# A state-space layer on Trainium2: next quarter's layer norm and half its input projection recorded inside the scan

## What is computed

```python
x = x + mamba(layernorm(x))        # state-space layer
x = x + ffn(layernorm(x))          # binarized weights
x = x + attn(layernorm(x))         # 16 x 16 scores of heads, per position
x = x + ffn(layernorm(x))

def mamba(x):                      # one sequence: 2048 x 1024
    xb, zb = split(x @ in_proj_w)  # 2048 x 2048 each
    xb = silu(causal_conv4(xb) + conv_b); zb = silu(zb)
    dt, B, C = split(xb @ x_proj_w)            # 128, 16, 16 wide
    dt = softplus(dt @ dt_proj_w + dt_proj_b)
    h[t] = exp(dt*A) * h[t-1] + dt*B[t]*xb[t]  # 2048 channels, 16 states each
    y = sum over states of h*C, plus xb*D
    return (y * zb) @ out_proj_w
```

## Time and profile before

| | us |
|---|---|
| median of 2 timed runs | 7102.89 (7080.65 and 7125.14) |
| profiled execution, slowest core | 7031.2 |
| its span, first to last instruction | 7029.7 (the eight cores 6995.0 to 7029.7) |
| VectorE busy | 3376.6 (48%) |
| TensorE matmul busy | 2594.3 (37%) |
| ScalarE busy | 1388.7 (20%) |
| GpSimd busy | 389.4 (6%) |

### The profile page before, as it was taken

The page is one execution under the profiler, slowest core; times in us unless marked ns, Lnnn a source line. Parts: engine busy times, 40 slices in busy tenths (PEclk is TensorE's granted clock), DMA queues, the critical chain, the costliest instruction groups (busy, mean ns, idle before and its releaser), DMA issues.

```text
span 7029.7 us, 35317 instructions; the slowest of 8 cores (6995.0 to 7029.7 us)
## 1 busy us (share of the span) xinstructions
PE 2594.3 (37%) x9120; PEld 935.0 (13%) x9120; DVE 3376.6 (48%) x3380; ACT 1388.7 (20%) x2282; POOL 389.4 (6%) x204
## 2 busy tenths in 40 slices
PE   3211115111134111152111200397833433436978
PEld 1000002000011000010000000143311111112433
DVE  0377771577753677735777640101155565563011
ACT  1122221222222222212222202212010100101120
POOL 1000000000000000000000011000002212211000
PEclk8655558555557555576555555698966666667989
DMA  6300005000011000021000069632400000001414
GB/s 111 65 0 0 0 0 92 29 0 0 0 27 45 24 0 0 0 55 41 0 0 0 19 106 118 89 75 45 87 0 0 0 0 0 0 0 22 81 41 109
DMA packets 691335, 226.16 MB, mean 32 GB/s; under 512 B 680122, under 2 KB 680253, under 8 KB 687552
## 3 DMA queue, kind: packets, MB, share of 16 engines
q1 hardware_dynamic: 555552, 168.14, 10.4%
q0 software_dynamic: 135584, 55.76, 7.0%
HBM read 241.73 MB, written 37.88 MB: 40 GB/s over the span
## 4 chain that ended last, share of the span: by engine, by line
DVE 39%; PE 25%; ACT 14%; DMA 12%; issue 6%; DVEq 2%; POOL 1%; ACTq 0%; SPq 0%; POOLq 0%; PEldq 0%
DVE AR L640 17%; ACT AR L613 10%; PE ps L881 6%; PE ps L851 5%; DVE AR L626 5%; DVE AR L1018 4%; DVE AR L1058 3%; DVE AR L1011 2%; DVE AR L492 2%; PE ps L1086 2%; PE ps L985 2%; PE ps L464 2%; PE ps L301 2%; DMA AR<-ip_bf 2%; DMA AR<-w 1%
## 5 line engine op out<-in xcount | busy, mean ns | idle before, releaser
L665 PE MATMUL ps<-AR 128*128 128x512 bf16 x1024 | 517.8, 608 | 2468.8 <-DVE AR L656 2468.8
L640 DVE TENSOR_TENSOR_SCAN AR<-AR 128x1024 bf16<-128x1024 f32 x512 | 1173.5, 2292 | 40.7 <-issue 3.8
L613 ACT ACTIVATE AR<-AR 128x511 f32<-128x511 f32 x1024 | 674.0, 705 | 1.1 <-issue 0.8
L626 DVE TENSOR_TENSOR AR<-AR 128x1024 bf16<-128x1024 bf16 x512 | 354.6, 693 | 485.2 <-ACT AR L613 485.2
L851 PE MATMUL ps<-AR 128*128 128x512 bf16 x2048 | 457.5, 384 | 126.1 <-DVE AR L336 111.7
L649 ACT ACTIVATE AR<-AR 128x2 f32<-128x2 bf16 x512 | 104.7, 204 | 1924.6 <-DVEq L63 1924.6
L1086 PE MATMUL ps<-AR 128*128 128x512 bf16 x512 | 220.7, 587 | 659.8 <-POOL AR L1072 635.0
L665 PEld LDWEIGHTS ps<-AR 128*128 128x128 bf16 x1024 | 70.0, 104 | 2915.0 <-issue 2915.0
L888 DVE TENSOR_SCALAR AR<-ps,AR 128x1024 f32<-128x1024 f32 x32 | 43.0, 1344 | 861.8 <-PE ps L881 861.8
L881 PE MATMUL ps<-AR 128*128 128x512 bf16 x2048 | 449.8, 383 | 12.7 <-DMA AR<-w2s 12.7
L656 DVE TENSOR_TENSOR AR<-AR 128x1024 bf16<-128x1024 bf16 x512 | 354.3, 692 | 127.7 <-issue 127.7
(11 more groups left out here) (92 smaller groups left out, 2340.6 us busy)
## 6 DMA issues: line engine op xcount, KB each, us to landing
AR<-w1s SPq DMA_DIRECT2D x128, 256.0 KB, 3.0
AR<-w2s SPq DMA_DIRECT2D x32, 1024.0 KB, 6.6
AR<-ip_bf SPq DMA_DIRECT2D x96, 256.0 KB, 2.9
AR<-bc_hbm SPq DMA_DIRECT2D x4, 4096.0 KB, 12.0
AR<-op_bf SPq DMA_DIRECT2D x24, 512.0 KB, 4.3
X<-x_fm SPq DMA_DIRECT2D x1, 8192.0 KB, 28.6
AR<-in_proj_w POOLq DMA_DIRECT2D x32, 256.0 KB, 5.2
ip_bf<-AR SPq DMA_DIRECT2D x32, 256.0 KB, 3.0
```

The source lines that it names most:

```text
L613: nbase=nbase: e.activation(out=dec_all[gb][:, n, 1:TQ], in_=dt[b][:, 1:TQ], func=AF.Exp, scale=av[:, dd, nbase + n:nbase + n + 1]),
L626: e.tensor_tensor(out=inp_all[0], in0=v[b].unsqueeze(1) .broadcast_to([128, G, TQ]), in1=bbc[:, nbase:nbase + G, :], op=ALU.mult))
L640: e.tensor_tensor_scan(out=h_all[hb].rearrange("p a b -> p (a b)"), data0=dec_all[gb].rearrange("p a b -> p (a b)"), data1=inp_all[0].rear ...
L665: e.matmul(self.bank(b, TQ), self.ident[:], hc_all[hb][:, n, :], start=(ng == 0 and n == 0), stop=(ng == NG - 1 and n == G - 1)),
```

## The change

The body of `_mamba` is divided into functions: `do_ln`, `inproj_block`, `do_conv`, `do_xproj`, `do_scan`, `do_outproj`. Quarter 0 is led in by layer norm, all 32 projection blocks, convolution and x-projection. Then, for each quarter q, the scan of q is recorded together with a list of "pieces": the layer norm of quarter q+1 and its projection blocks 0 to 15, 17 pieces in all. After each `groups(dd-1)` two pieces are recorded. After the scan come output projection q, projection blocks 16 to 31 of q+1, its convolution and x-projection. The barrier at the end of each quarter is gone; one stands at the end of the stage. Waits name the counts that they need. The rest follows from that or is small:

- Layer norm takes its scratch from xbpre instead of the tile of B and C, and accumulates in banks 4 and 5; dt and v get memory of their own; the gated output is written over zbs, and g is gone; x-projection uses bank 5 instead of 6.
- TensorE's wait for the small weights (x_proj_w, dt_proj_w) moves to the begin of the stage.
- The wait for the broadcast load (d_spb) moves from ahead of the scan into each group; the prologue gets a wait xbs_ready, the end of a channel block zb_ready, each projection block xn_ready. For the first two blocks of each projection half SP waits for its own last DMA on the buffer (sp_par).
- Drains are removed: in layer norm, after L730 and L895, in the weight preparation, and in attention after L1018, L1058 and ahead of three increments (`r.inc` has a drain of its own).
- In attention the tiles sc, am, sm get two buffers each instead of one.

```diff
-    def _layernorm(self, t0, tlen, xn_view, o_ln):
+    def _layernorm(self, t0, tlen, xn_view, o_ln, bb=0, bb2=2, waits=None):
...
-        o_g = o_xbpre
...
-        o_dt = o_xn
-        o_v = o_xn + 2 * TQ * 4
+        o_dt = alloc(2 * TQ * 4)
+        o_v = alloc(2 * TQ * 2)
...
-        o_ln = o_bbc
+        o_lnm = o_xbpre
...
         r.wait("gp", "d_gpb", small_w)
+        r.wait("pe", "d_gpb", small_w)
...
+        def do_ln(qq):
+            lv = max(st.get("ln_ve", 0), st.get("conv_ve", 0))
+            ln_waits = [("act", "c_ve", lv), ("pe", "c_ve", lv)]
+            self._layernorm(qq * TQ, TQ, xn, o_lnm, bb=4, bb2=5,
+                            waits=ln_waits)
+            st["xn_ready"] = r.cnt["c_ve"]
+            st["ln_ve"] = r.cnt["c_ve"]
+            st["ln_evac"] = r.cnt["c_act"]
+
+        def inproj_block(qq, m, mm_done, ev_done, wr_done, dst):
+            b = m % 2
+            if qq == 0:
...
+            else:
+                if m >= 2:
+                    r.wait("sp", "c_pe", mm_done[m - 2])
+                if m in (0, 1, 16, 17):
+                    r.wait("sp", dsem("sp", b), st["sp_par"][b])
+                ddone = r.op("sp", lambda e, m=m, b=b: e.dma_start(
+                    out=wi[b], in_=d["ip_bf"][:, m * 128:(m + 1) * 128]
+                    .rearrange("(k p) f -> p k f", p=128)),
+                     inc=dsem("sp", b), inck=16)[dsem("sp", b)]
+                st["sp_par"][b] = ddone
+                r.wait("pe", dsem("sp", b), ddone)
+            r.wait("pe", "c_ve", st["xn_ready"])
+            if m >= 2:
+                r.wait("pe", "c_act", ev_done[m - 2])
+            else:
+                r.wait("pe", "c_act", st["ln_evac"])
+                r.wait("pe", "c_ve", st["ln_var"])
+            for k in range(8):
+                c = r.op("pe", lambda e, m=m, b=b, k=k: e.matmul(
+                    self.bank(4 + b, TQ), wi[b][:, k, :], xn[:, k, :],
+                    start=(k == 0), stop=(k == 7)),
+                         inc="c_pe" if k == 7 else None)
+            mm_done[m] = c["c_pe"]
+            r.wait("act", "c_pe", mm_done[m])
+            if m < 16:
+                c = r.op("act", lambda e, m=m, b=b: e.activation(
+                    out=xbpre[:, m, 3:3 + TQ], in_=self.bank(4 + b, TQ),
+                    func=AF.Copy), inc="c_act")
+            else:
+                r.wait("act", "c_pe", st.get("op_mm", 0))
...
-            bc_done = r.cnt["d_spb"]
-            r.wait("gp", "d_spb", bc_done)
-            r.wait("ve", "d_spb", bc_done)
-            r.wait("pe", "c_act")
...
             def prologue(dd):
...
                 r.wait("ve", "c_act", dt_ev[b])
-                if dd >= 2:
-                    r.wait("ve", "c_gp", inp_done[(dd - 2, NG - 1)])
+                r.wait("ve", "c_act", xbs_ready)
...
             def groups(dd):
...
                     r.wait("ve", "c_act", dec_done[key])
-                    inp_done[key] = r.cnt["c_gp"]
+                    r.wait("ve", "d_spb", bc_done)
                     if dd + ng > 0:
                         sem, val = hc_done.get(keyp2, ("c_ve", 0))
                         r.wait("ve", sem, val)
...
                 r.wait("ve", "c_pe", ymm_done[(dd, NG - 1)])
+                r.wait("ve", "c_act", zb_ready)
...
-                ep_done = r.op("ve", lambda e, dd=dd, b=b: e.tensor_tensor(
-                    out=g[:, dd, :], in0=yv[b], in1=zbs[:, dd, :],
+                ep_done[0] = r.op("ve", lambda e, dd=dd, b=b: e.tensor_tensor(
+                    out=zbs[:, dd, :], in0=yv[b], in1=zbs[:, dd, :],
                     op=ALU.mult), inc="c_ve")["c_ve"]
...
                     prologue(dd)
                 if dd >= 1:
                     groups(dd - 1)
...
-                r.drain("ve")
-            r.barrier()
+                for _ in range(2):
+                    if pieces:
+                        pieces.pop(0)()
+            while pieces:
+                pieces.pop(0)()
+            return ep_done[0]
+
...
+        do_ln(0)
+        st["ln_var"] = r.cnt["c_ve"]
+        mm0, ev0, wr0 = [0] * 32, [0] * 32, [0] * 32
+        for m in range(32):
+            inproj_block(0, m, mm0, ev0, wr0, None)
+        do_conv(0)
+        do_xproj(0)
+        for q in range(4):
+            pieces = []
+            if q < 3:
...
+                pieces.append(mk_ln())
+                for m in range(16):
...
+                    pieces.append(mk_ip())
+            ep = do_scan(q, pieces)
+            do_outproj(q, {"ep": ep})
+            if q < 3:
+                qq = q + 1
+                for m in range(16, 32):
+                    inproj_block(qq, m, mmw, evw, wrw, None)
+                do_conv(qq)
+                do_xproj(qq)
+        r.barrier()
...
-        sc = [self.view(o_s, F32, [128, 16, 16]) for i in (0, 1)]
-        am = [self.view(o_a, BF16, [128, 16, 16]) for i in (0, 1)]
-        sm = [self.view(o_sm, F32, [128, 16]) for i in (0, 1)]
+        sc = [self.view(o_s + i * 1024, F32, [128, 16, 16]) for i in (0, 1)]
+        am = [self.view(o_a + i * 512, BF16, [128, 16, 16]) for i in (0, 1)]
+        sm = [self.view(o_sm + i * 64, F32, [128, 16]) for i in (0, 1)]
...
                 cv = r.op("ve", lambda e, b=b, jg=jg, jb2=jb2: e.reduce_sum(
                     out=sc[b][0:U, :, 2 * jg:2 * jg + 2].transpose([0, 2, 1]),
                     in_=ot[jb2][0:U], axis=AX.X), inc="c_ve")["c_ve"]
-                r.drain("ve")
```

More of the change, by code:

```diff
@@ L291, in _layernorm @@
         t1 = self.view(o_ln, F32, [128, tlen])
-        r.wait("act", "c_ve")
+        nsl = cdiv(tlen, 512)
+        if waits is None:
+            r.wait("act", "c_ve")
+        else:
+            for eng, sem, val in waits:
+                r.wait(eng, sem, val)
         r.op("act", lambda e: e.activation(out=xsq, in_=self.Xv[:, :, tsl],
                                            func=AF.Square), inc="c_act")
-        nsl = cdiv(tlen, 512)
-        r.wait("pe", "c_act")
-        r.wait("pe", "c_ve")
+        if waits is None:
+            r.wait("pe", "c_act")
+            r.wait("pe", "c_ve")
+        else:
+            r.wait("pe", "c_act")
         for ns in range(nsl):
@@ L311, in _layernorm @@
         r.op("act", lambda e: e.activation(
-            out=mean_sb, in_=self.pair(0, tlen), func=AF.Copy), inc="c_act")
+            out=mean_sb, in_=self.bank(bb, tlen) if tlen <= 512 else
+            self.pair(bb, tlen), func=AF.Copy), inc="c_act")
         r.wait("ve", "c_act")
@@ L316, in _layernorm @@
         r.drain("ve")
[L317 to L320, removed]
-        r.drain("ve")
+        r.op("ve", lambda e: e.tensor_tensor(
+            out=rstd_sb,
+            in0=self.bank(bb2, tlen) if tlen <= 512 else self.pair(bb2, tlen),
+            in1=rstd_sb, op=ALU.subtract), inc="c_ve")
         r.wait("act", "c_ve")
@@ L416, in _mamba @@
         r.wait("gp", "d_gpb", small_w)
[L418 to L423, removed]
+        r.wait("pe", "d_gpb", small_w)
+        st = {}
+        def do_ln(qq):
[6 more added lines that the diff above has]
+            st["ln_evac"] = r.cnt["c_act"]
@@ L479, in _mamba @@
-            r.wait("ve", "c_act")
             silu_done = [0] * 16
@@ L506, in _mamba, with do_xproj @@
                  inc="c_ve")
-            r.drain("ve")
-            r.wait("pe", "c_act")
-            r.wait("pe", "d_gpb", small_w)
+            st["xbs_ready"] = silu_done[15]
+            st["conv_ve"] = r.cnt["c_ve"]
+        def do_xproj(qq):
+            r.wait("pe", "c_act", st["xbs_ready"])
             for k in range(16):
@@ L552, in _mamba @@
             ymm_done = {}
-            ep_done = 0
+            ep_done = [0]
             G = 2
             NG = NST // G
+            bc_done = st["bc_done"]
+            dtraw_ready = st["dtraw_ready"]
+            xbs_ready = st["xbs_ready"]
+            zb_ready = st["ip_ev"]
             def prologue(dd):
@@ L560, in prologue @@
                     r.wait("pe", "c_act", dt_ev[b])
+                else:
+                    r.wait("pe", "c_act", dtraw_ready)
                 cpe = r.op("pe", lambda e, dd=dd, b=b: e.matmul(
```

241 lines of the change are left out of this document (116 added, 125 removed).

## The result

The changed kernel takes 7004.22 us in the median of 27 runs (6974.48 to 7156.11), the kernel before on the same chips 7055.06 us in 26 (7029.17 to 7177.43). The ratio is 0.9905, with a 95% interval of 0.9882 to 0.9929: about 1% faster, a small gain and a sure one. (Some executions of every kernel here take some per cent longer, with a lower granted clock on the cores of one die or of both; the medians are of all executions, the ratios of those without it.) My forecast was 0.2% slower. The profiled execution has a span of 6983.3 us against 7029.7.

What follows compares the result with a forecast made beforehand. VectorE holds 39% of the 7029.7 us span, TensorE 25%; between channel blocks TensorE, ScalarE and VectorE stand in series. Terms sum to +13.5 us: 7116 by the median of 7102.89, range 7030 to 7180.

Steps and rivals of the forecast that it cites:

- Projection pairs: Between the scan's channel blocks: each pair of projection blocks lies in series, 6.2 us; three quarters 152 against 128, +24 us.
- bound for a pair without a rise: Passages between channel blocks: 16 matmuls that never see the clock rise take 6.7 us, from eight at 3.36.
- Attention: Score passes and softmax handover: removed drains save 17 us (10 to 21), at 0.09 to 0.17 us each after L1018.
- Waits: VectorE in the scan: each added satisfied wait costs 0.065 us; +33 us in groups, +4 in the prologue.
- waits free: Rival for the scan's added waits: they cost nothing, rest as summed, 7077 us; chance 0.28 together with rival 2.
- rival 2: Added waits cost nothing and removed drains save nothing: -8.5 us, 7094; chance 0.28 together with rival 3.
- Broadcast load, barriers, layer norm: First stage: layer norm moved at 0 covers the broadcast load, -40 us; removed barriers -3, a late store +2.
- Small weights: Start of the stage: TensorE's wait for them moves ahead of layer norm's matmuls, +8.5 us once.
- Double buffers in attention, stages costed at nothing: Attention's double buffers, in-place gating, moved buffers and blocks 16 to 31 cost 0; chance of an unseen stage moving 0.08.
- Real overlap: Rival: projection hides under VectorE in the scan, -138 us, 6965; chance 0.07.
- Late weights: Rival: a projection block's load starts only at its turn, +70 to +139 us, 7186 to 7255; chance 0.05.

Runs made afterwards that it cites:

- m2: Changed kernel with one piece recorded after each channel block instead of two; state-space stage 3955.4 us, 17 us more.
- m3: Changed kernel with all 17 pieces recorded behind the scan, none inside; state-space stage 3951.6 us against 3938.2.
- m4: Changed kernel with projection blocks 0 to 15 recorded inside the scan's loop, ScalarE's copy two groups later; ratio to the kernel before 0.9714.
- a3: Changed kernel with the last softmax product repeated three times more in each attention pass; attention 1148.9 us, ratio to the kernel before 0.9962.
- a5: Changed kernel with the last softmax product repeated seven times in each attention pass; attention 1152.6 us.
- m1: Changed kernel with the scan's three added waits recorded once a scan; ratio to the kernel before 0.9842, state-space stage 3907.7 us.
- a1: Changed kernel with all removed drains of attention put back; attention 1150.5 us, ratio to the kernel before 0.9951.

## Why the prediction was wrong

Two steps of the prediction failed, the size of the projection pairs and a term of attention that it did not have. Direction: I forecast 0.2% slower, it is 1% faster. In absolute numbers 48 of the 112 us between 7116 and 7004.22 are the base: the two timed runs of before that I added to have median 7102.89, and 26 runs have 7055.06. The rest is two terms.

- **Projection pairs, the mis-sized term.** Forecast 6.2 us each. The scans grew by 145 us in all; loops (29) and plain passages (8) make 37 of it, block 15 makes 3 x 2.95, and 99 remain for 21 pairs, 4.74 us each. The mechanism was right (series, order, TensorE and ScalarE, nothing hidden; the load ready; m2, m3, m4). 21 x 1.45 = 31 us, all of the miss in this stage. I took 5.9 us for the matmuls, from two rows of 5.50 and 6.52 us, in which TensorE had idled 16.7 us and 54 us before, and added 0.3 for copy and waits. In the passages they took 4.5 to 6.2 us, 4.8 in the median, and the 0.3 does not show: where they took 4.80, the passage is 4.55 over the plain one. Here TensorE comes from a loop in which it works every 5.2 us; that this makes them cheaper is argued and not tested, and it is not the whole, as the same surroundings gave 4.5 and 6.2. My bound for a pair without a rise was too low as well: the eight matmuls of 3.36 us have a granted clock of 0.55, and eight at 0.50 throughout take 3.62 (m2).
- **Attention, the missing term.** Forecast -17, measured -49. The drain was bounded at 0.09 to 0.17 us and costs 0.185: 6 us more than the 15 I took. The other 26 are the clock of the next projection (13 more passages at 13.6 instead of 15.6 us), which I put at nothing: I priced a removed instruction by its own gap, and took the rest of the pass as fixed. That the change gained them is luck of its timing: a3 and a5 show that 1.5 us more a pass takes them away and 3.5 us gives them back.
- **Waits.** Forecast 33 + 4, measured 29 + 8 = 37. The rival "waits free" falls by m1. What the Trainium skill says in VectorE: DVE Perf Modes, section "The DRAIN you can't avoid", is that a semaphore after each instruction costs nothing extra; I read it as speaking of waits too, and a wait instruction behind a late one was 0.065 us here. The same section has it that the flush between VectorE instructions can't be skipped by leaving out semaphores. It means the pipeline's own flush, so rival 2, in which the explicit drains can't be saved, does not follow from it; the rows of L1018 and L1091 show 0.185 us for an explicit drain that was taken out. (The advice to keep instructions few rather than semaphores stands in the Trainium skill, VectorE: DVE Perf Modes, section "Rules for kernel authors".)
- **Broadcast load, barriers, layer norm.** Gaps and start together: forecast -177 + 29 = -148, measured on core 0 -182 + 37 = -145. Of the terms in them the load is told apart: its cover in three scans is 22 us by m3, forecast 20, and the fourth scan's wait is 5.7 us on core 0 over the 1.1 for ScalarE (8.9 on core 3), forecast 5.6 (10.5 - 4.9). Barriers and layer norm are not, and the agreement of the sum does not prove each.
- **Small weights.** Forecast 8.5, measured 12.2 - 3.9 = 8.3.
- **Double buffers in attention, stages costed at nothing.** 0 by a1; the two stretches behind the first stage moved by -3 and -2.
- **Rivals.** Real overlap did not happen (m3: the scans lose 112 us, and the rest takes about as much more), though the idle time was there to be had, in another place (m4). Late weights did not happen: the blocks of the passages ran without a wait for DMA.

## What to carry to other kernels

Work that is moved "into" a busy stage hid here only where it was recorded inside the loop whose idle time it is to use, on each engine in turn: TensorE's block behind the sums, ScalarE's copy behind the exponentials. Between two loops it was paid in full, 108 us (21 pairs and block 15 three times) against none. Leave a wait out of an inner loop once its event has been waited for by the same engine. And before pricing an edit in a loop with TensorE bursts, look at the granted clock of every burst in it: shortening one engine's part moved TensorE's clock here, and that was worth more than what was cut (26 us against 23).

## What the runs showed of the hardware

- In a periodic attention pass TensorE's projection met the high clock at 71.7 us a pass, the low one at 75.1, and the high one again with 3.3 us more work, at 75.0: removing 1.4 us from a pass saved 3.3, adding 1.5 cost 3.2. Why is open.
- A satisfied wait on VectorE's list cost 0.065 us behind the one that ends last; one explicit drain between two long VectorE instructions cost 0.185 us (0.09 of gap and 0.09 of overlap lost).
- Sixteen matmuls of 128x512 right behind sums that come every 5.2 us took 4.5 to 6.2 us, 4.8 in the median of 21; after 17 us of idle time they took 5.5, after 54 us 6.5, once each.
